# Output projection in eight matmuls instead of nine: the third block's high part stands twice in its stationary tile

## The reference

```
q = heads(x @ Wq)                                   # x: 128 x 128 x 320
h_s = softmax(q k_s^T / 4) v_s  for the 4 segments s # k_s, v_s from ctx: 128 x 128 x 512
out = merge(h_txt + h_obj + h_oth + h_ip) @ Wo + bo + x
```

## Time and profile before

| | |
|---|---|
| median of three runs | 1628.12 us |
| profiled execution, its own time | 1628.05 us |
| its span, first to last instruction | 1625.8 us |
| mean granted TensorE clock | 0.992 of full speed |
| busy over the span: PE, PEld | 97%, 87% |
| busy over the span: DVE, ACT, POOL | 86%, 78%, 89% |
| chain that ended last, largest shares | POOL 63%, issue 21%, PE 7%, DVE 4% |
| POOL L566, low part of the output, x128 | 1005 ns each, 128.7 us |

### The profile page before, as it was taken

How to read it: one execution, slowest core, us unless ns; L and a number is a source line. 1 busy time by engine, 2 the same in 40 slices (tenths; PEclk the granted TensorE clock), 3 DMA queues, 4 the chain that set the end, 5 groups by cost and what they waited for, 6 DMA issues and landing times.

```text
span 1625.8 us, 51529 instructions
## 1 busy us (share of the span) xinstructions
PE 1572.4 (97%) x16252; PEld 1419.1 (87%) x16252; DVE 1400.4 (86%) x3359; ACT 1266.2 (78%) x2416; POOL 1447.6 (89%) x1646
## 2 busy tenths in 40 slices
PE   6969999999999999999999999999999999999976
PEld 3668999999999999999999999999999999999965
DVE  3348989888898988889898889989888998988896
ACT  1238888888888888888888888888888888888764
POOL 3359999999999999999999999999999999999865
PEclk9989999999999999999999999999999999999999
DMA  9678899889989988998998899899889989988861
GB/s 318 157 207 210 232 251 240 217 242 231 220 240 248 240 219 238 230 223 237 249 239 219 240 228 221 240 251 241 218 237 227 222 241 250 235 223 237 212 144 34
DMA packets 423237, 366.26 MB, mean 225 GB/s; under 512 B 19041, under 2 KB 394274, under 8 KB 418850
## 3 DMA queue, kind: packets, MB, share of 16 engines
q1 hardware_dynamic: 423202, 365.80, 86.3%
HBM read 216.38 MB, written 149.34 MB: 225 GB/s over the span
## 4 chain that ended last, share of the span: by engine, by line
POOL 63%; issue 21%; PE 7%; DVE 4%; POOLq 1%; DMA 1%; SPq 1%; ACT 1%; ACTq 0%
POOL probs L527 31%; POOL whole L495 9%; POOL x_lo L516 7%; POOL parts L501 5%; POOL probs L530 5%; POOL oT L566 4%; POOL c L508 2%; PE ring_ps L894 2%; DVE l_seg L806 1%; DVE probs L779 1%; DVE m_seg L763 1%; PE job_ps L943 1%; PE job_ps L930 1%; PE job_ps L934 1%; PE ring_ps L1021 1%
## 5 line engine op out<-in xcount | busy, mean ns | idle before, releaser
L527 POOL TENSOR_TENSOR probs<-probs,rl 128x616 f32<-128x616 f32 (+1 forms) x640 | 629.0, 1004 | 44.1 <-DVE rl L817 43.7
L806 DVE TENSOR_REDUCE l_seg<-probs 128x8 f32<-128x616 f32 (+1 forms) x640 | 386.2, 645 | 80.8 <-ACT probs L645 77.6
L657 ACT ACTIVATE pT<-ring_ps 128x512 f32<-128x512 f32 x640 | 382.3, 605 | 72.5 <-PE ring_ps L1021 68.6
L1021 PE MATMUL ring_ps<-ident,probs 128*128 128x128 f32 x2560 | 391.1, 278 | 10.9 <-DVE y_all L828 7.8
L779 DVE TENSOR_TENSOR probs<-s_ps,m_seg 128x616 f32<-128x616 f32 (+1 forms) x640 | 387.5, 648 | 0.0
L763 DVE TENSOR_REDUCE m_seg<-s_ps 128x8 f32<-128x616 f32 (+1 forms) x640 | 371.5, 623 | 3.5 <-issue 0.2
L645 ACT ACTIVATE probs<-probs 128x1024 f32<-128x1024 f32 x320 | 342.7, 1071 | 6.7 <-DVE probs L783 6.7
L1021 PEld LDWEIGHTS ring_ps<-ident,probs 128*128 128x128 f32 x2560 | 291.5, 144 | 44.6 <-issue 25.2
L943 PE MATMUL job_ps<-c,w 128*128 128x312 f32 x1860 | 305.1, 313 | 0.9 <-POOL c L508 0.9
L943 PEld LDWEIGHTS job_ps<-c,w 128*128 128x128 f32 x1860 | 272.8, 190 | 1.3 <-POOL c L508 1.3
L930 PE MATMUL job_ps<-c_in,w 128*128 128x172 f32 x1280 | 217.9, 313 | 6.5 <-DMA c_in<-in_cT 5.4
(11 more groups left out here) (69 smaller groups left out, 2064.0 us busy)
## 6 DMA issues: line engine op xcount, KB each, us to landing
q_all<-q_scratch SPq DMA_DIRECT2D x64, 960.0 KB, 7.5
k_all<-k_scratch SPq DMA_DIRECT2D x64, 960.0 KB, 11.7
c_in<-in_cT SPq DMA_DIRECT2D x32, 1024.0 KB, 5.2
x_raw<-in_xT SPq DMA_DIRECT2D x32, 768.0 KB, 7.2
q_scratch<-parts SPq DMA_DIRECT2D x64, 384.0 KB, 6.0
k_scratch<-parts SPq DMA_DIRECT2D x64, 384.0 KB, 5.3
x_res<-in_x SPq DMA_DIRECT2D x128, 160.0 KB, 4.5
out<-y_all SPq DMA_DIRECT2D x128, 160.0 KB, 3.8
```

What stands on the lines that cost most here:

```text
L527: pool.tensor_tensor(pr[:, :, a:e], pr[:, :, a:e], r[:, :, s:s + 1].broadcast_to((P, OH, e - a)), ALU.mult)
L657: act.activation(pT[:, h:h + QH, :], ring_ps[i][:, :].rearrange("p (h s) -> p h s", h=QH), ACT.Copy)\
L806: dve.tensor_reduce(l_seg[:, o % 2, :, s:s + 1], pr[:, :, a:e], axis=AX.X, op=ALU.add)
L1021: last = pe.transpose(ring_ps[i][:, k * S:(k + 1) * S], probs[:, (o % NR) * OH + q * QH + k, :], ident[:, :])
```

## The change

The third block's 64 empty rows are filled. In `oT[0]` the high part of block three stands twice, in rows 0 to 63 and again in rows 64 to 127; `w_o[0]` holds the high weights in the upper rows and the low weights in the lower ones, so one matmul gives high x high and high x low. The second matmul takes `oT[1]`, the low part above, and below it a constant with ones in rows 64 and 96, against high weights above and the bias below, in a high and a low piece. So a batch has eight matmuls. ACT makes three casts for a batch where it made one (128x256, then 64x128 twice), POOL two subtractions where it made one (128x256 and 64x128).

The constant pieces are made once, before the loop. The zeros and ones stand in the tile `x_res`, the bias in `oT_raw`; four ACT copies (two of them new weights' pieces, one the bias, one the ones) now come ahead of the third group's x casts, and two DVE subtractions follow the first `shift`. SP's first residual load waits for the first of the four copies, since it overwrites the ones; DVE waits for all four.

```
...
             def load_res(b, i):
 
+                if isinstance(b, int) and b == 0:
+                    sp.wait_ge(wo_hi_made, 1)
                 sp.dma_start(x_res[:, i, :], x[b]).then_inc(res_loaded[i], 16)
...
-            sp.dma_start(wo_raw[0:CT, 2, :], wo[2 * P:C, :]).then_inc(w_o_loaded, 16)
+            for at in (0, CT):
+                sp.dma_start(wo_raw[at:at + CT, 2, :], wo[2 * P:C, :]).then_inc(w_o_loaded, 16)
             sp.wait_ge(pads_made, N_PADS - 1)
-            sp.dma_start(wo_raw[CT:CT + 1, 2, :], bo.rearrange("(a c) -> a c", a=1)).then_inc(w_o_loaded, 16)
+            for at in (0, P - 32 - CT):
+                sp.dma_start(b_rows[at:at + 1, :], bo.rearrange("(a c) -> a c", a=1)).then_inc(w_o_loaded, 16)
...
-            pool.wait_ge(wo_hi_made, 1)
-            pool.tensor_tensor(w_o[1][:, :, :], wo_raw[:, :, :], w_o[0][:, :, :].bitcast(fp32), ALU.subtract)\
+            pool.wait_ge(wo_hi_made, 4)
+            pool.tensor_tensor(w_o[1][:, 0:2, :], wo_raw[:, 0:2, :], w_o[0][:, 0:2, :].bitcast(fp32), ALU.subtract)\
                 .then_inc(wo_lo_made, 1)
 
             def oT_low(b):
 
                 pool.wait_ge(oT_hi_made, b + 1)
-                pool.tensor_tensor(oT[1][:, :, :], oT_raw[:, :, :], oT[0][:, :, :].bitcast(fp32), ALU.subtract)\
+                pool.tensor_tensor(oT[1][:, 0:2, :], oT_raw[:, 0:2, :], oT[0][:, 0:2, :].bitcast(fp32), ALU.subtract)
+                pool.tensor_tensor(oT[1][0:CT, 2, :], oT_raw[0:CT, 2, :], oT[0][0:CT, 2, :].bitcast(fp32), ALU.subtract)\
                     .then_inc(oT_lo_made, 1)
...
             def oT_high(b):
 
                 act.wait_ge(oT_copied, b + 1)
-                act.activation(oT[0][:, :, :], oT_raw[:, :, :], ACT.Copy).then_inc(oT_hi_made, 1)
+                act.activation(oT[0][:, 0:2, :], oT_raw[:, 0:2, :], ACT.Copy)
+                act.activation(oT[0][0:CT, 2, :], oT_raw[0:CT, 2, :], ACT.Copy)
+                act.activation(oT[0][CT:P, 2, :], oT_raw[0:CT, 2, :], ACT.Copy).then_inc(oT_hi_made, 1)
...
             spread(0, 1)
+            act.wait_ge(w_o_loaded, 16 * 5)
+            act.wait_ge(ones_made, 2)
+            act.activation(oT[1][CT:P, 2, :], ones_rows, ACT.Copy).then_inc(wo_hi_made, 1)
+            act.activation(w_o[1][CT:P, 2, :], b_rows, ACT.Copy).then_inc(wo_hi_made, 1)
+            act.activation(w_o[1][0:CT, 2, :], wo_raw[0:CT, 2, :], ACT.Copy).then_inc(wo_hi_made, 1)
+            act.activation(w_o[0][:, :, :], wo_raw[:, :, :], ACT.Copy).then_inc(wo_hi_made, 1)
             for k in range(CX):
                 x_high(2, k)
-            act.wait_ge(w_o_loaded, 16 * 3)
-            act.activation(w_o[0][:, :, :], wo_raw[:, :, :], ACT.Copy).then_inc(wo_hi_made, 1)
...
             shift(0, 0)
+            at = P - 32
+            dve.wait_ge(wo_hi_made, 4)
+            dve.tensor_tensor(w_o[0][CT:P, 2, :], wo_raw[CT:P, 2, :], w_o[0][CT:P, 2, :].bitcast(fp32), ALU.subtract)\
+               .then_inc(b_lo_made, 1)
+            dve.tensor_tensor(w_o[1][at:at + 1, 2, :], b_rows[at - CT:at - CT + 1, :],
+                              w_o[1][at:at + 1, 2, :].bitcast(fp32), ALU.subtract).then_inc(b_lo_made, 1)
...
-                for k in range(3):
+                for k in range(2):
                     for a, c in ((0, 0), (0, 1), (1, 0)):
-                        last = pe.matmul(ring_ps[i][:, 0:C], oT[a][:, k, :], w_o[c][:, k, :],
-                                         start=(k == 0 and (a, c) == (0, 0)), stop=(k == 2 and (a, c) == (1, 0)))
+                        pe.matmul(ring_ps[i][:, 0:C], oT[a][:, k, :], w_o[c][:, k, :],
+                                  start=(k == 0 and (a, c) == (0, 0)), stop=False)
+                for a in range(2):
+                    last = pe.matmul(ring_ps[i][:, 0:C], oT[a][:, 2, :], w_o[a][:, 2, :], start=False, stop=(a == 1))
                 last.then_inc(y_filled, 1)
...
```

More of the change, by code:

```diff
@@ L41 @@
 N_CONSTS = 3
-N_PADS = 6
+N_PADS = 5
 SEQ = [("kv", 3), ("kv", 4), ("q", 0), ("v", 0), ("q", 1), ("v", 1), ("q", 2), ("v", 2), ("kv", 0), ("v", 3),
@@ L210, in xattn_kernel @@
         wo_raw = y_all[:, 0:3 * C].rearrange("p (k c) -> p k c", k=3)
+        b_rows = oT_raw[:, :, :].rearrange("p k s -> p (k s)")[CT:P, 0:C]
+        ones_rows = x_res[CT:P, 0, 0:S]
         v_flat = v_pad[:, :, :, :].rearrange("p b h w -> p (b h w)")
@@ L228, in xattn_kernel @@
         ident_made = sem("ident_made")
+        ones_made = sem("ones_made")
         x_loaded = sem("x_loaded")
@@ L272, in xattn_kernel @@
         wo_lo_made = sem("wo_lo_made")
+        b_lo_made = sem("b_lo_made")
         y_filled = sem("y_filled")
@@ L660, in copy_oT @@
             def copy_oT(b, i):
+                if isinstance(b, int) and b == 0:
+                    act.wait_ge(b_lo_made, 2)
                 act.wait_ge(pv_filled, b + 1)
@@ L832, in _ @@
             dve.memset(q_all[KS:P, 0:H * 2 * S].bitcast(fp32), 0.0).then_inc(pads_made, 1)
[L833 to L836, removed]
+            dve.memset(b_rows, 0.0).then_inc(pads_made, 1)
+            dve.memset(ones_rows, 0.0).then_inc(pads_made, 1)
+            dve.wait_ge(pads_made, N_PADS - 1)
+            for at in (CT, P - 32):
+                dve.memset(x_res[at:at + 1, 0, 0:S], 1.0).then_inc(ones_made, 1)
             def copy_small(n):
@@ L1040, in project @@
                     pe.wait_ge(wo_lo_made, 1)
+                    pe.wait_ge(b_lo_made, 2)
                 pe.wait_ge(oT_lo_made, b + 1)
-                for k in range(3):
+                for k in range(2):
                     for a, c in ((0, 0), (0, 1), (1, 0)):
-                        last = pe.matmul(ring_ps[i][:, 0:C], oT[a][:, k, :], w_o[c][:, k, :],
-                                         start=(k == 0 and (a, c) == (0, 0)), stop=(k == 2 and (a, c) == (1, 0)))
+                        pe.matmul(ring_ps[i][:, 0:C], oT[a][:, k, :], w_o[c][:, k, :],
+                                  start=(k == 0 and (a, c) == (0, 0)), stop=False)
+                for a in range(2):
+                    last = pe.matmul(ring_ps[i][:, 0:C], oT[a][:, 2, :], w_o[a][:, 2, :], start=False, stop=(a == 1))
                 last.then_inc(y_filled, 1)
```

## The result

| | before | after |
|---|---|---|
| median, us (lowest to highest, runs) | 1627.95 (1627.56 to 1630.01, 4) | 1638.47 (1637.68 to 1639.46, 4) |
| ratio, 95% interval | 1 | 1.006 [1.0048, 1.0072] |
| span of the profiled execution, us | 1625.8 | 1636.6 |
| first transposes of the loop (PE) begin, us | 115.00 | 121.76 |
| period of a group, us | 47.452 | 47.576 |

The forecast was 1636.7 us. The period is the distance between the same projection early and late in the span, divided by the turns between. The span grew by 10.8 us, in three places.

A forecast was written before the change was run, and what follows sets the result against it. The prediction took a loop PE, ACT, POOL, ACT, with a period of 47.45 us, to bound the kernel. Start 6.2, clock 1, loop 1.2 and end 0.2 gave +8.6 on 1628.05: 1636.7 us, own range 1629 to 1646.

The forecast's parts named there:

- The mechanism: A closed loop PE, ACT, POOL, ACT sets the group period of 47.45 us; SP's new wait delays the start.
- signs named ahead: Expected trace readings, among them three casts holding ACT 0.7 us, two subtractions POOL 1.0, first transposes at 120 to 122.5.
- The start: Ahead of the loop: `x_raw` queues behind residual loads waiting for ACT, delaying PE's first transposes; +6.2 us.
- The clock: At the start: PE's longer idle stretch makes more time at half speed likelier, 0 to +3 us, taken as +1.
- The loop: Per group of four batches: +0.32 + 0.03 - 0.31 = +0.04 us, some 29 turns, +1.2 us.
- PE: forecast -0.31: Loop's PE piece: one matmul less in each of two projections, -0.31 us per group; the other two give nothing.
- ACT: forecast +0.32: Loop's ACT piece: three casts instead of one, 0.73 us against 0.41, delay POOL by +0.32 us per group.
- POOL: forecast +0.03: Loop's POOL piece: two subtractions instead of one, little fixed cost per instruction, +0.03 us per group.
- The end: Last batch's cast, subtraction and projection with nothing beside them: +0.32 + 0.03 - 0.157 = +0.2 us.
- PE-bound: Rival, whole kernel: each of the 128 saved matmuls counts, -20.1 us, giving 1615 us; chance 0.11.
- POOL-bound: Rival, every batch: POOL and ACT set the time, PE's saving gives nothing, 1657 us; chance 0.13.
- The covered start: Rival, start: the load lands early enough or the middle absorbs its delay, no change, 1629.5 us; chance 0.08.

The follow-up runs named there:

- e1: Changed kernel with SP's load of the third group's x and the key-part stores moved ahead of the two residual loads: 1633.44 us, ratio 1.0030.
- e2: Kernel before with eight projection matmuls per batch, leaving out high part times low weights of the third block, nothing else changed: 1614.69 us, ratio 0.9916.
- e3: Kernel before, nine matmuls, with three casts (the third into rows 64 to 127 of a spare tile) and two subtractions: 1645.47 us, ratio 1.0105.
- e5: Kernel before with three casts only, the third into rows 0 to 63 of a spare tile: 1639.31 us, one run.
- e4: Kernel before with POOL's subtraction in two instructions and nothing else changed: 1632.99 us, ratio 1.0027.
- e8: Changed kernel, x load ahead of residual loads; POOL's first subtraction released after ACT's first cast, its second after the second cast: 1617.86 us, ratio 0.9936.
- e6: Changed kernel with POOL released after ACT's second cast, the third cast having its own semaphore for PE: 1628.28 us, ratio 0.9998.

## Why the prediction was right, step by step

The mechanism held in both places, and the time came out 1.8 us above the forecast. That the sum came so close is in part luck: the loop came out 2.4 us dearer than forecast and the clock 1 us cheaper, and inside the loop three errors of 0.09 to 0.13 us a turn partly cancel. Two of the signs named ahead came out otherwise by the same terms: three casts hold ACT for 0.95 us (945.74 to 946.69) and not 0.7, two subtractions hold POOL for 1.11 (946.74 to 947.85) and not 1.0.

*The start: +6.2 forecast, +6.8 measured.* `x_raw` went out at 106.47 (106.4 forecast), landed in the upper half of the range given, and the first transposes fell at 121.76, inside 120 to 122.5. e1 shows the cause.

*The clock: +1 forecast, about 0 measured.* PE was idle for 7.47 us, three times as long as before. The clock was at 0.99 until 118.00 and at 0.50 until 124.70; so it fell while PE stood still, and was back 3.0 us after the first transposes (124.7 - 121.76). Before it was 3.1 us (118.1 - 115.00). The term took a longer stretch at half level for time lost, though 2.5 of its 6.7 us (118.00 to 120.49) lay where PE had no work. From the first transposes to the second PE took 3.73 us (121.76 to 125.49), before 3.79 (115.00 to 118.79).

*The loop: +0.04 per turn forecast, +0.124 measured.* Three sizes were wrong, and partly cancelled.

- PE: forecast -0.31 for the two projections in its piece of the loop. e2 gives -0.44. The sentence "the other two of a group fall where PE waits for the loop, and give nothing" failed for one of them: it stands beside ACT's piece, in which a copy waits for PE, and so comes through as ACT's -0.15 (-0.16 in e2, where ACT's own work is unchanged).
- ACT: forecast +0.32, measured +0.41 at POOL's release. The duration of a small cast (0.26 to 0.31) was right; that 0.1 of it overlaps with its neighbour was not: the third cast writes from row 64 on, and there the overlap is lost (e3 against e5).
- POOL: forecast +0.03, measured +0.14 (e4: +0.14 per turn). The step was the comparison of 128x384 with 128x256 in the earlier trace rows. The two differ in more than their columns: the first writes the rounded type from float operands (L566), the second plain float with one bfloat16 operand (L495, `parts`). So their difference was no price of 128 columns; which of the types makes it, no run shows. Of one kind, the rows after are:

```profile
L574 POOL TENSOR_TENSOR oT<-oT_raw,oT x92: 712/733/756, 306.2 to 1386.0; 128x256 fp32r<-128x256 f32 x92
L575 POOL TENSOR_TENSOR oT<-oT_raw,oT x92: 445/456/478, 306.9 to 1386.7; 64x128 fp32r<-64x128 f32 x92
```

(durations in ns, min/median/max). 128 columns are 733 - 456 = 277 ns, so 456 - 277 = 179 ns are fixed, or 0.15 us where starts are compared (0.69 and 0.42). The old 128x384 lies on the same line: 179 + 3 x 277 = 1010 ns, and it lasted 1005 in the mean.

*The end: +0.2 forecast, +0.5 measured.* From the first cast to the projection's start the last batch takes 0.54 us more (1619.68 to 1621.42 before, 1630.00 to 1632.28 now), the same misjudged casts and subtractions; from there to the residual addition only 0.06 is given back (1.60 and 1.54), not 0.157.

*The rivals.* PE-bound falls by e2 (period 47.01, not 46.8) and by e3, where added ACT and POOL work appears in full. POOL-bound falls by e2 too: with POOL's work unchanged the period fell. The covered start falls by the 6.29 us of waiting. That the period rose by so little is a balance of +0.56 and -0.44, and not a sign that the edits lie hidden; e2 and e3 show the two halves apart.

Left open: how much of e8's period is still ACT's, and whether its four copies at the start can be moved behind the first exponential. Neither was tried.

## What to carry to other kernels

In a periodic kernel follow one small recurring wait around until it closes, and price an edit by the piece of that loop it stands in; a saving counts on the engine's neighbours too, where these wait for it. Before splitting an instruction that another engine waits for, ask which part that engine really needs, and release it there: here that was worth 0.33 + 0.18 = 0.51 us per turn (e6, e8), more than the 0.44 of the matmul saved (e2). And when a price is taken from two rows, let them differ in one thing only, the types of output and operands included.

## What the runs showed of the hardware

- ACT's neighbouring instructions overlap by about 0.1 us where they begin at the same partition (a cast of 0.30 us, the next start 0.20 later, e5), and hardly where that changes from 0 to 64 or back (0.30 to 0.34 from start to start, e3 and the kernel after). Only these two first rows occur here. The Trainium skill, "ScalarE: Activation LUTs", section "What ACT_TABLE_LOAD costs", gives an overlap of some 93 ns between neighbours; e5 agrees with it, the starts in e3 do not.
- POOL's subtractions into the rounded type cost 0.15 to 0.18 us an instruction and 2.16 ns a column (277 ns per 128), an estimate from the medians of two sizes, 456 and 733 ns, that a third, 1005 ns for 384 columns, fits. One more instruction in the loop cost 0.14 us a turn (e4).
- After a longer idle time of PE (7.47 us, before 2.48) the clock was back from the half level no later: 4.2 us after the first scores (120.49 to 124.7), before 4.4 (113.69 to 118.1). This is one execution each.
